# A two-layer pixelwise kernel: column stage in two 64x64 tiles, and regions of 13 row tiles for 15

## The chip, the cores and the metric

The kernel runs on one core of a Trainium2 chip. The metric is the device time of one execution in microseconds (us), lower is better. Engines are named as the profile names them: PE (TensorE matmuls), PEld (its weight loads), DVE (VectorE), ACT (ScalarE), POOL (GpSimd), SP (SyncE, which here only issues DMAs).

## What is computed

```
x: (1, 16, 1024, 1024)                      # 16 channels, rows t, columns s, float32
# first layer: a bias that depends on the distance t - s alone
rel  = tril(t - s)
nd   = log(|c * rel| + 1) / (log(|c * max(rel_max(t), threshold)| + 1) + 1e-6)
bias = relu(nd * W1 + b1) @ W2 + b2         # 32 hidden values to 16 channels
y    = x + bias
# second layer: channel mixing, part of it by row, part by column
A[t] = w + I + sum_i qw1[t,i] (x) qw2[t,i] + diag(qdd[t])     # 16 x 16 for each row t
B[s] =         sum_i kw1[s,i] (x) kw2[s,i] + diag(kdd[s])     # 16 x 16 for each column s
out[:, t, s] = A[t]^T y[:, t, s] + B[s]^T y[:, t, s]
```

## The kernel before

**Layout.** The 1024 columns are 8 blocks of W = 128. The 128 partitions are 8 blocks times 16 channels, in four groups of 32: two blocks' channels interleaved (GS = 2). A *row tile* is 8 rows by all columns, 128 x 1024 values; there are 128. Row tiles are taken in 9 *regions* of 8 and then 15 tiles (`REGION_TILES`). The buffer `homes` has three homes of 15 tiles: x of one region is loaded one tile behind the place where y is then written, and the mixed result of a region goes into another home.

**Work of a region k**, in steps:

- 16 *column tiles* (`b_columns`, L736): 8 columns each. For each column a 16x16 matrix acts on the 120 rows of the region. Two blocks' matrices stand as a 32x32 block-diagonal weight in `mats_b`, one matmul for each of the four groups, at the array's four diagonal 32x32 tiles: 32 matmuls of 32x32 weights and 120 columns to a column tile. Float32 makes each matmul two records in the profile, each with a weight load.
- then 15 *row tiles* (`a_rows`, L723), the same with the row's matrices from `mats_a`, 32 matmuls of 128 columns.
- in between, at the steps that `bias_step` gives (about every second), one *bias tile* (`bias_tile`, L747) of region k + 1: the hidden values of 8 rows, which GpSimd multiplies (L451) and ScalarE passes through Relu (L490), times W2, four matmuls of 512 columns with one hidden tile (first half of the rows) and eight records, so twice as many, with two.

Column sums are written out of the PSUM tile `main` by ScalarE on even steps (`take_b`, L517) and VectorE on odd ones (L629), row results are added by VectorE (`finish_tile`, L639), and VectorE adds the bias to x (`add_bias`, L657); in the first half of the rows ScalarE does half of the x partitions (L501). `main` has two halves, so TensorE can be at most two tiles ahead of those who empty it. Each engine runs its program strictly as written.

**The queues.** SP issues all loads of x, in pieces (`LOAD_PIECES`, 15 tiles as 1, 3, 3, 3, 4, 1, numbered from 0, each as 8 DMAs, one for each block), the row matrices (`load_mats_a`, four DMAs, which wait until GpSimd has spread an earlier set, L428), and half of the stores (`store_upper`, four DMAs of a piece of `STORE_PIECES`, behind the last row tile of the piece). ScalarE issues the other half of the stores. What stands in SP's program in the loop over k and T (L374 to L397): pieces 3 and 4 of region k + 1 first; then, by row tile T of region k, a_mats, piece 5 of region k + 1 at T = 6, the stores, and pieces 0, 1, 2 of region k + 2 at T = 7, 10, 13. An instruction that waits holds up all behind it.

**Start.** b's matrices are made by VectorE, transposed by TensorE, written out by SP and loaded back into `mats_b` (L336), which ScalarE fills with zeros before (L484).

Of the kernel before, what the change touches and what calls it, by code (L numbers as in the profile page):

```python
# [5 lines left out]
ACT = mybir.ActivationFunctionType  # L6

P = 128
H = 16
S = 1024  # L10
W = 128
BLOCKS = S // W
GS = 2
GROUPS = BLOCKS // GS
GP = H * GS
HID = 32
SLOTS = P // HID
ROWS = 8
COLS = ROWS * W
COL_TILES = W // ROWS  # L20
BANK = 512
REGION_TILES = (8,) + (15,) * 8
REGIONS = len(REGION_TILES)
FIRST_TILE = [sum(REGION_TILES[:k]) for k in range(REGIONS)]
ALL_TILES = S // ROWS
HALF_TILES = ALL_TILES // 2
HOME_TILES = max(REGION_TILES)
HOMES = 3
STORE_PIECES = {8: (2, 3, 3), 15: (2, 3, 3, 3, 4)}
LAST_STORES = (2, 3, 3, 3, 2, 1, 1)  # L30
LOAD_PIECES = {8: (1, 3, 4), 15: (1, 3, 3, 3, 4, 1)}
PORTIONS = (2, 2)
CHUNK = 32
CHUNK_TILES = CHUNK // ROWS
# [6 lines left out]
RING = 3  # L41
# [12 lines left out]
def build(nc, x, W1, b1, W2, b2, c, L_mult, init_L, qw1, qw2, kw1, kw2, qdd, kdd, w, out):  # L54
# [6 lines left out]
    with ExitStack() as ctx:  # L61
        def sb(name, shape):
            return ctx.enter_context(nc.sbuf_tensor(name, shape, F32))

        def sem(name):
            return ctx.enter_context(nc.semaphore(name))
# [2 lines left out]


        homes = sb("homes", [P, HOMES * HOME_TILES * COLS])
        mats_b = sb("mats_b", [P, GS * H * W])


        mats_in = sb("mats_in", [P, A_RING * H * CHUNK])
# [10 lines left out]
        zero_col = sb("zero_col", [P, 1])  # L86
# [53 lines left out]
        y_const_ready = sem("y_const_ready")  # L140
        main_ready = sem("main_ready")
        main_taken = [sem(f"main_taken{i}") for i in range(2)]
        out_done = [sem(f"out_done{i}") for i in range(len(LAST_STORES))]

        def tile_of(k, T):
            return FIRST_TILE[k] + T
# [1 line left out]
        def groups_of(u):  # L148
            return 1 if u < HALF_TILES else 2
# [70 lines left out]
        def load_pieces(k):  # L220
            return LOAD_PIECES[REGION_TILES[k]]

# [9 lines left out]
        def y_slot(k, T):  # L232
            return k % HOMES * HOME_TILES + T
# [24 lines left out]
        def of_block(tensor, pitch, b, offset, dims):  # L258
            start = (b // GS) * GP + b % GS
            return bass.AP(tensor, start * pitch + offset, [[GS * pitch, H]] + dims)  # L260
# [38 lines left out]
        def _(sp):  # L299
# [33 lines left out]

            def load_mats_b():
                for b in range(BLOCKS):
                    sp.dma_start(of_block(mats_b, GS * H * W, b, b % GS * W, [[GS * W, H], [1, W]]),  # L336
                                 b_mats[b]).then_inc(b_in, DMA)

            def save_mats(part):
# [18 lines left out]
            load_x(0, 2)  # L358
            save_mats("b")
            sp.wait_ge(mats_out["b"], 2 * DMA)  # L360
            sp.wait_ge(mats_zeroed, 1)
            load_mats_b()
            for i in range(3):
                load_x(1, i)
# [8 lines left out]
            loaded = [3, 5] + [0] * (REGIONS - 2)  # L373
            for k in range(REGIONS):  # L374

                while k + 1 < REGIONS and loaded[k + 1] < 5:
                    load_x(k + 1, loaded[k + 1])
                    loaded[k + 1] += 1
                if k == 2:
                    sp.wait_ge(scales_out, DMA)  # L380
                    sp.wait_ge(nd_ready, PART // 2 // ROWS)
                    sp.dma_start(row_scale[:, 0:PART // 2], late_scales[:, 0:PART // 2]).then_inc(scales_in, DMA)
                if k == 4:
                    sp.wait_ge(nd_ready, PART // ROWS)
                    sp.dma_start(row_scale[:, PART // 2:], late_scales[:, PART // 2:]).then_inc(scales_in, DMA)
                for T in range(REGION_TILES[k]):
                    v = chunk_behind(tile_of(k, T))
                    if v is not None:
                        load_mats_a(v)
                    if k + 1 < REGIONS and T == min(6, REGION_TILES[k] - 4):  # L390
                        load_x(k + 1, 5)
                    for i in range(len(store_pieces(k))):
                        if T == piece_start(store_pieces(k), i + 1) - 1 - (i == 4 and k < REGIONS - 1):
                            store_upper(k, i)
                    if k + 2 < REGIONS and T in (7, 10, 13):
                        load_x(k + 2, loaded[k + 2])
                        loaded[k + 2] += 1  # L397
            for i in range(len(out_done)):
# [3 lines left out]
        def _(pool):  # L402
# [30 lines left out]
            for u in range(ALL_TILES):  # L433
                t0 = u * ROWS
                if t0 == W:
                    pool.wait_ge(tables_made, 2)
                if t0 == PART:
                    pool.wait_ge(scales_in, DMA)
                if t0 == PART + PART // 2:
                    pool.wait_ge(scales_in, 2 * DMA)  # L440
                for g in range(groups_of(u)):
                    h = hidden_index(u, g)

                    while h >= RING and spread < UNITS and place_of_unit(spread) <= place_of_bias(tile_of_hidden[h - RING]):
                        spread_unit(spread)
                        spread += 1
                    if h >= RING:
                        pool.wait_ge(hidden_used, h - RING + 1)
                    logs = log_table[:, t0 - SLOTS * W * g:t0 - SLOTS * W * g + ROWS]
                    scales = row_scale[:, t0 % PART:t0 % PART + ROWS]  # L450
                    nc.gpsimd.tensor_tensor(  # L451
                        hidden_tile(u, g).rearrange("p (j s) -> p j s", j=ROWS),
                        bass.AP(logs.tensor, logs.offset, [list(logs.ap[0]), [1, ROWS], [1, W]]),
                        bass.AP(scales.tensor, scales.offset, [list(scales.ap[0]), [1, ROWS], [0, W]]),
                        ALU.mult).then_inc(nd_ready, 1)
# [5 lines left out]
        def _(act):  # L461
# [17 lines left out]
            for part in (row_scale[:, W:], scale_late):  # L479
# [1 line left out]
            act.wait_ge(w1_in, 2 * DMA)  # L481
            act.wait_ge(table_loaded, 1)
            nc.scalar.activation(relu_b1[:], b1_col[:], ACT.Relu).then_inc(relu_b1_made, 1)
            nc.scalar.activation(mats_b[:], zero_col[:].to_broadcast([P, GS * H * W]), ACT.Copy)\  # L484
                .then_inc(mats_zeroed, 1)

            def make_hidden(u):
# [193 lines left out]
        def _(pe):  # L681
# [19 lines left out]
            def of_group(g):  # L701
                return slice(GP * g, GP * (g + 1))

            def staggered(j, g):

                return (j + (ROWS // 2) * (g % 2)) % ROWS
# [2 lines left out]
                pitch = 2 * A_UNIT  # L709
                return bass.AP(mats_a, GP * g * pitch + w % 2 * A_UNIT + row, [[pitch, GP], [UNIT, GP]])  # L710

            def b_weights(g, col):
                return bass.AP(mats_b, GP * g * GP * W + col, [[GP * W, GP], [W, GP]])

            def y_row(k, T, g, j):
                at = y_slot(k, T) * COLS + j // 2 * 2 * W
                return homes[of_group(g), at:at + 2 * W].rearrange("p (s b) -> p s b", b=2)[:, :, j % 2]

            def y_column(k, g, col):
                rows = homes[of_group(g), y_slot(k, 0) * COLS:y_slot(k, REGION_TILES[k]) * COLS]  # L720
                return rows.rearrange("p (j s b) -> p j s b", s=W, b=2)[:, :, col, :]

            def a_rows(k, T):  # L723
# [12 lines left out]
            def b_columns(k, C):  # L736
                i = b_tile(k, C)
                taken, count = emptied(i - 2)
                pe.wait_ge(taken, count)
                for n in range(ROWS):  # L740
                    for g in range(GROUPS):
                        j = staggered(n, g)
                        mm = pe.matmul(main[of_group(g), i % 2, j * W:j * W + REGION_TILES[k] * ROWS],  # L743
                                       b_weights(g, C * ROWS + j), y_column(k, g, C * ROWS + j), start=True, stop=True)
                mm.then_inc(main_ready, 1)

            def bias_tile(u):  # L747
# [58 lines left out]
```

## Time and profile before

| | us |
|---|---|
| median of 3 runs | 911.75 |
| lowest and highest | 904.46, 914.53 |
| span of the profiled execution, first to last instruction | 930.2 |
| TensorE busy in it | 741.4 |
| GpSimd, VectorE, ScalarE busy | 432.9, 452.3, 387.6 |
| DMA traffic | 149.63 MB, 161 GB/s on average |

The profiled execution has no time of its own in the list beside its span. The span is 18.5 us over the median of the runs. Shares of the span are averages over stages with different limits. "issue" as the reason of an idle time means that the engine waited for nothing that the profile shows.

### The profile page before, as it was taken

How to read it: one execution, taken by the hardware profiler on the slowest of the kernel's cores; microseconds unless marked ns; L12 is line 12 of the kernel's file. 1: busy time of each engine (PE TensorE's matmuls, PEld its weight loads, DVE VectorE, ACT ScalarE, POOL GpSimd, SP SyncE). 2: the span in 40 equal slices, each digit the busy share in tenths (PEclk: the TensorE clock that was granted, in tenths of full speed). 3: DMA queues.
4: the chain of work that ended last, by engine and by line, in shares of the span. 5: the costliest groups of instructions: out<-in, count | busy, mean ns of one | idle time of the engine just before them, and what ended most of it. 6: DMA issues, size and time to landing. Idle time of an engine off the chain costs nothing. (4 is left out here: it accounts for less than half of the span.)

```text
span 930.2 us, 39085 instructions
## 1 busy us (share of the span) xinstructions
PE 741.4 (80%) x18210; PEld 547.7 (59%) x18210; DVE 452.3 (49%) x483; ACT 387.6 (42%) x412; POOL 432.9 (47%) x267
## 2 busy tenths in 40 slices
PE   0678864798678876898799978999689878897984
PEld 0255654576556655666557745677357645676974
DVE  7496522376345533564346524464336524464352
ACT  3958624553463435543433334344233342341200
POOL 3545421254233432365458745586358753581020
PEclk9888887999999999999999999999899988999997
DMA  6787687658975999587976898488875988589068
GB/s 132 183 172 140 147 180 167 145 100 190 194 180 125 183 184 201 124 183 161 223 156 129 174 181 192 94 172 172 182 162 110 199 178 151 106 176 227 5 155 200
DMA packets 301055, 149.63 MB, mean 161 GB/s; under 512 B 30045, under 2 KB 296669, under 8 KB 300893
## 3 DMA queue, kind: packets, MB, share of 16 engines
q1 hardware_dynamic: 231456, 113.56, 56.9%
q10 hardware_dynamic: 69436, 33.58, 17.0%
q8 instruction: 143, 2.34, 1.1%
q14 instruction: 20, 0.16, 0.1%
HBM read 77.61 MB, written 69.47 MB: 158 GB/s over the span
## 5 line engine op out<-in xcount | busy, mean ns | idle before, releaser
L451 POOL TENSOR_TENSOR hidden<-log_table,row_scale 128x1024 f32<-128x1024 f32 x192 | 365.4, 1917 | 367.4 <-PE bias L757 359.5
L743 PE MATMUL main<-homes,mats_b 32*32 32x120 f32 (+1 forms) x9216 | 286.5, 272 | 119.6 <-issue 83.3
L743 PEld LDWEIGHTS main<-homes,mats_b 32*32 32x32 f32 x9216 | 257.9, 133 | 187.5 <-issue 136.1
L490 ACT ACTIVATE hidden<-hidden,b_col 128x1024 f32<-128x1024 f32 x192 | 220.3, 1149 | 310.3 <-POOL hidden L451 205.1
L732 PEld LDWEIGHTS main<-homes,mats_a 32*32 32x32 f32 x8192 | 238.1, 129 | 78.6 <-issue 54.9
L732 PE MATMUL main<-homes,mats_a 32*32 32x128 f32 x8192 | 258.8, 275 | 23.7 <-issue 23.6
L657 DVE SCALAR_TENSOR_TENSOR homes<-bias,b_col,homes 64x512 f32<-64x512 f32 (+1 forms) x256 | 185.8, 747 | 174.9 <-DMA homes<-in_x 106.5
L757 PE MATMUL bias<-hidden,w_blocks 128*64 128x512 f32 x768 | 207.6, 648 | 17.7 <-DVE b_col L620 8.8
L639 DVE TENSOR_TENSOR homes<-main,homes 128x1024 f32<-128x1024 f32 x128 | 156.8, 1225 | 107.7 <-PE main L732 104.6
L629 DVE COPY homes<-main 128x960 f32<-128x960 f32 x64 | 74.1, 1157 | 179.7 <-PE main L743 179.5
L517 ACT ACTIVATE homes<-main 128x960 f32<-128x960 f32 (+1 forms) x80 | 71.1, 891 | 109.4 <-PE main L743 99.3
L428 POOL TENSOR_TENSOR mats_a<-mats_in,own_block 128x512 f32<-128x512 f32 x64 | 66.5, 1040 | 107.4 <-PE main L732 96.7
L501 ACT ACTIVATE homes<-homes,b_col 64x512 f32<-64x512 f32 x128 | 89.4, 749 | 64.5 <-DMA homes<-in_x 54.1
L757 PEld LDWEIGHTS bias<-hidden,w_blocks 128*64 128x64 f32 x768 | 46.4, 143 | 86.6 <-issue 74.6
L697 PE MATMUL bias<-relu_b,w_blocks 128*64 128x1 f32 x2 | 0.3, 241 | 15.1 <-DVE w_blocks L614 15.1
L290 DVE TENSOR_TENSOR homes<-homes 128x2048 f32<-128x2048 f32 x4 | 10.6, 2698 | 0.1
L697 PEld LDWEIGHTS bias<-relu_b,w_blocks 128*64 128x64 f32 x2 | 0.3, 204 | 15.1 <-issue 15.1
L691 PE MATMUL main<-homes 128*128 128x128 f32 x32 | 6.5, 389 | 3.0 <-DVE homes L594 3.0
L691 PEld LDWEIGHTS main<-homes 128*128 128x128 f32 x32 | 5.9, 206 | 4.8 <-DVE homes L594 3.2
L589 DVE TENSOR_TENSOR homes<-homes 128x2048 f32<-128x2048 f32 x2 | 6.2, 3110 | 0.1
L509 ACT ACTIVATE homes<-main 128x1024 f32<-128x1024 f32 x4 | 4.1, 1025 | 2.1 <-PE main L691 2.1
L473 ACT ACT_TABLE_LOAD x1 | 1.3, 1283 | 7.5 <-issue 7.5
(37 smaller groups left out, 32.2 us busy)
## 6 DMA issues: line engine op xcount, KB each, us to landing
homes<-in_x SPq DMA_DIRECT2D x200, 192.0 KB, 6.5
out_mixed<-homes ACTq DMA_DIRECT2D x104, 192.0 KB, 5.9
out_mixed<-homes SPq DMA_DIRECT2D x104, 192.0 KB, 5.6
homes<-in_x SPq DMA_DIRECT2D x72, 256.0 KB, 7.1
homes<-in_x SPq DMA_DIRECT2D x136, 64.0 KB
mats_in<-a_mats SPq DMA_DIRECT2D x128, 64.0 KB
out_mixed<-homes ACTq DMA_DIRECT2D x28, 256.0 KB, 8.0
out_mixed<-homes SPq DMA_DIRECT2D x28, 256.0 KB, 5.8
```

The source lines that it names most:

```text
L428: nc.gpsimd.tensor_tensor(mats_a[:, w % 2 * A_UNIT:(w % 2 + 1) * A_UNIT].rearrange("p (n b e) -> p n b e", n=H, b=GS), rows.unsqueeze(2).t ...
L451: nc.gpsimd.tensor_tensor(hidden_tile(u, g).rearrange("p (j s) -> p j s", j=ROWS), bass.AP(logs.tensor, logs.offset, [list(logs.ap[0]), [1 ...
L490: nc.scalar.activation(hidden_tile(u, g), hidden_tile(u, g), ACT.Relu, bias=b1_col[:, 0:1])\
L501: add = nc.scalar.activation(y_rows(high_half, k, T, b), x_rows(high_half, k, T, b), ACT.Identity, bias=b2_col[high_half, 1:2])
L517: nc.scalar.activation(mixed_columns(k, C), column_sums(k, C), ACT.Copy)\
L629: dve.tensor_copy(mixed_columns(k, C), column_sums(k, C)).then_inc(main_taken[b_tile(k, C) % 2], 1)
L639: dve.tensor_tensor(at, main[:, i % 2, :], at, ALU.add).then_inc(main_taken[i % 2], 1)
L657: add = dve.scalar_tensor_tensor(out=y_rows(rows, k, T, b), in0=falling(u, b, 0 if both else b * (P // 2), P if both else P // 2), scalar= ...
L691: mm = pe.transpose(main[:, i % 2, b * P:(b + 1) * P], comp[part][:, at:at + P], ident)
L732: mm = pe.matmul(main[of_group(g), i % 2, j * W:(j + 1) * W], a_weights(g, w, part * ROWS + j), y_row(k, T, g, j), start=True, stop=True)
L743: mm = pe.matmul(main[of_group(g), i % 2, j * W:j * W + REGION_TILES[k] * ROWS], b_weights(g, C * ROWS + j), y_column(k, g, C * ROWS + j), ...
L757: mm = pe.matmul(bias[into, u % 2, b * BANK:(b + 1) * BANK], w2_blocks[:, g, :], rows, start=True, stop=True)
```

## The change

The column stage works on four blocks at a time. `mats_b` holds 64x64 block-diagonal matrices (two groups' blocks, 4 x 16 channels), twice as large, and a column tile is 16 matmuls of 64x64 weights at the array's two diagonal 64x64 tiles. The row stage stays at 32x32. A home has 13 tiles: the regions are 6, nine times 13, and 5 tiles, eleven in all, with load and store pieces to match. ScalarE fills one half of `mats_b` with zeros as before, GpSimd the other half, ahead of its fourth hidden tile, and the load of the matrices waits for both. The second scale load stands at region 5 for 4.

```diff
+QS = 4
+QUADS = BLOCKS // QS
+QP = H * QS
-REGION_TILES = (8,) + (15,) * 8
+REGION_TILES = (6,) + (13,) * 9 + (5,)
-STORE_PIECES = {8: (2, 3, 3), 15: (2, 3, 3, 3, 4)}
-LAST_STORES = (2, 3, 3, 3, 2, 1, 1)
-LOAD_PIECES = {8: (1, 3, 4), 15: (1, 3, 3, 3, 4, 1)}
+STORE_PIECES = {6: (2, 2, 2), 13: (2, 3, 3, 3, 2)}
+LAST_STORES = (2, 1, 1, 1)
+LOAD_PIECES = {6: (1, 2, 3), 13: (1, 3, 3, 3, 2, 1), 5: (1, 2, 2)}
...
-        mats_b = sb("mats_b", [P, GS * H * W])
+        mats_b = sb("mats_b", [P, QP * W])
...
-                    sp.dma_start(of_block(mats_b, GS * H * W, b, b % GS * W, [[GS * W, H], [1, W]]),
+                    sp.dma_start(of_block(mats_b, QP * W, b, (b % QS // GS * GP + b % GS) * W, [[GS * W, H], [1, W]]),
...
-                while k + 1 < REGIONS and loaded[k + 1] < 5:
+                while k + 1 < REGIONS and loaded[k + 1] < min(5, len(load_pieces(k + 1))):
...
-                if k == 4:
+                if k == 5:
...
-                    if k + 1 < REGIONS and T == min(6, REGION_TILES[k] - 4):
+                    if k + 1 < REGIONS and len(load_pieces(k + 1)) > 5 and T == min(6, REGION_TILES[k] - 2):
...
-                    if k + 2 < REGIONS and T in (7, 10, 13):
+                    if k + 2 < REGIONS and T in (7, 10, 12):
...
+                if u == RING:
+                    nc.gpsimd.memset(mats_b[:, GP * W:], 0.0).then_inc(mats_zeroed, 1)
...
-            nc.scalar.activation(mats_b[:], zero_col[:].to_broadcast([P, GS * H * W]), ACT.Copy)\
+            nc.scalar.activation(mats_b[:, 0:GP * W], zero_col[:].to_broadcast([P, GP * W]), ACT.Copy)\
...
-            def b_weights(g, col):
-                return bass.AP(mats_b, GP * g * GP * W + col, [[GP * W, GP], [W, GP]])
+            def b_weights(q, col):
+                return bass.AP(mats_b, QP * q * QP * W + col, [[QP * W, QP], [W, QP]])
...
-                    for g in range(GROUPS):
-                        j = staggered(n, g)
-                        mm = pe.matmul(main[of_group(g), i % 2, j * W:j * W + REGION_TILES[k] * ROWS],
-                                       b_weights(g, C * ROWS + j), y_column(k, g, C * ROWS + j), start=True, stop=True)
+                    for q in range(QUADS):
+                        j = staggered(n, q)
+                        mm = pe.matmul(main[of_quad(q), i % 2, j * W:j * W + REGION_TILES[k] * ROWS],
+                                       b_weights(q, C * ROWS + j), y_column(k, q, C * ROWS + j), start=True, stop=True)
```

SP's program, before, from the a_mats load that stands ahead of piece 5 (`16x8x128 x8` is a piece of one tile) to pieces 2 and 3; row 65 is piece 1:

```order
59 L325 DMA mats_in<-a_mats 32x1x512 x4
60 L317 DMA homes<-in_x 16x8x128 x8
61 L268 DMA out_mixed<-homes 16x24x128 x4
62 L317 DMA homes<-in_x 16x8x128 x8
63 L325 DMA mats_in<-a_mats 32x1x512 x4
64 L268 DMA out_mixed<-homes 16x24x128 x4
65 L317 DMA homes<-in_x 16x24x128 x8
66 L325 DMA mats_in<-a_mats 32x1x512 x4
67 L268 DMA out_mixed<-homes 16x32x128 x4
68 L317 DMA homes<-in_x 16x24x128 x16
```

The same place in the changed program (line numbers are four higher); row 63 is piece 1:

```order
57 L272 DMA out_mixed<-homes 16x24x128 x4
58 L321 DMA homes<-in_x 16x8x128 x8
59 L329 DMA mats_in<-a_mats 32x1x512 x4
60 L272 DMA out_mixed<-homes 16x24x128 x4
61 L321 DMA homes<-in_x 16x8x128 x8
62 L272 DMA out_mixed<-homes 16x24x128 x4
63 L321 DMA homes<-in_x 16x24x128 x8
64 L329 DMA mats_in<-a_mats 32x1x512 x4
65 L272 DMA out_mixed<-homes 16x16x128 x4
66 L321 DMA homes<-in_x 16x24x128 x16
```

Between piece 5 and piece 1 the kinds and counts are the same; only the last store piece (row 67, now 65) is two tiles for four.

TensorE's program in a column stage, before (a row here is a matmul of the program, two records in the profile):

```order
70 L743 MATMUL main<-homes,mats_b 32x120 x64
71 L757 MATMUL bias<-hidden,w_blocks 64x512 x2
72 L743 MATMUL main<-homes,mats_b 32x120 x64
73 L757 MATMUL bias<-hidden,w_blocks 64x512 x2
74 L743 MATMUL main<-homes,mats_b 32x120 x64
```

and in the changed program, to the first row tile of the region:

```order
70 L752 MATMUL main<-homes,mats_b 64x104 x32
71 L766 MATMUL bias<-hidden,w_blocks 64x512 x2
72 L752 MATMUL main<-homes,mats_b 64x104 x32
73 L766 MATMUL bias<-hidden,w_blocks 64x512 x2
74 L752 MATMUL main<-homes,mats_b 64x104 x48
75 L766 MATMUL bias<-hidden,w_blocks 64x512 x2
76 L752 MATMUL main<-homes,mats_b 64x104 x16
77 L741 MATMUL main<-homes,mats_a 32x128 x32
```

Half as many matmuls stand between two bias tiles, and now and then three column tiles for two.

## Rows read from the trace of the kernel before

**Rows 1.** The page: engines, busy us; a DMA queue, packets, MB, share
```profile
PE 741.4 (80%) x18210; PEld 547.7 (59%) x18210; DVE 452.3 (49%) x483; ACT 387.6 (42%) x412; POOL 432.9 (47%) x267
...
q8 instruction: 143, 2.34, 1.1%
```

**Rows 2.** Windows: rows of region 5; columns of region 6; last rows
```profile
594.00:635.50 41.50, 41.50 (x1021) 30.51 (x1023) 28.43 (x30) 16.10 (x14) 35.40 (x22) 1.00 0.71 152
635.50:696.90 61.40, 49.12 (x1099) 32.65 (x1091) 20.17 (x23) 24.53 (x24) 28.42 (x16) 0.92 0.80 171
882.00:920.60 38.60, 30.95 (x961) 29.29 (x960) 18.31 (x15) 0.00 (x0) 6.24 (x6) 0.96 0.77 170
```

**Rows 3.** Timeline of TensorE in the last row stage
```profile
894.95 3.94 PE L732 MATMUL main<-homes,mats_a 32*32 32x128 f32 x127 [1.40 <-issue]
```

**Rows 4.** Waits: who for whom, us in total, times, longest
```profile
PE main L743 <- issue: 83.3, 45, 4.7
DVE homes L657 <- DMA homes<-in_x: 106.5, 13, 14.8
```

**Rows 5.** Timeline of VectorE: its second bias tile in four regions
```profile
155.39 1.51 DVE L657 SCALAR_TENSOR_TENSOR homes<-bias,b_col,homes 64x512 f32<-64x512 f32 x2 [7.20 <-DMA homes<-in_x]
...
453.06 1.41 DVE L657 SCALAR_TENSOR_TENSOR homes<-bias,b_col,homes 128x512 f32<-128x512 f32 x2 [10.30 <-DMA homes<-in_x]
...
660.69 1.41 DVE L657 SCALAR_TENSOR_TENSOR homes<-bias,b_col,homes 128x512 f32<-128x512 f32 x2 [14.80 <-DMA homes<-in_x]
...
765.83 1.41 DVE L657 SCALAR_TENSOR_TENSOR homes<-bias,b_col,homes 128x512 f32<-128x512 f32 x2 [13.85 <-DMA homes<-in_x]
```

**Rows 6.** Timeline of the SP queue: start, us, line, transfer, count
```profile
408.56 6.61 SPq L317 DMA_DIRECT2D homes<-in_x  x8
...
431.49 13.58 SPq L317 DMA_DIRECT2D homes<-in_x  x8
...
452.58 25.39 SPq L317 DMA_DIRECT2D homes<-in_x  x24
...
613.62 6.92 SPq L317 DMA_DIRECT2D homes<-in_x  x8
```

**Rows 7.** DMA of the stretch 431 to 478 us
```profile
DMA packets 17987, 9.17 MB, mean 195 GB/s; under 512 B 714, under 2 KB 17842, under 8 KB 17980
```

**Rows 8.** Timeline of TensorE in the column stage of region 4
```profile
431.07 3.64 PE L743 MATMUL main<-homes,mats_b 32*32 32x120 f32 x128
...
444.65 3.29 PE L743 MATMUL main<-homes,mats_b 32*32 32x120 f32 x116 [0.66 <-issue]
...
452.51 1.86 PE L743 MATMUL main<-homes,mats_b 32*32 32x120 f32 x60 [2.35 <-issue]
...
457.44 1.94 PE L757 MATMUL bias<-hidden,w_blocks 128*64 128x512 f32 x8
...
465.00 3.44 PE L757 MATMUL bias<-hidden,w_blocks 128*64 128x512 f32 x8
...
487.57 3.86 PE L732 MATMUL main<-homes,mats_a 32*32 32x128 f32 x128
```

**Rows 9.** Windows, TensorE: us, busy (records), clock, DMA share, GB/s
```profile
433.00:441.00 8.00, 6.85 (x190) 1.00 0.55 70
859.00:863.00 4.00, 3.83 (x80) 0.50 0.07 19
870.40:880.40 10.00, 10.00 (x397) 1.00 0.02 5
```

**Rows 10.** Timeline of TensorE: a column tile of 64 columns
```profile
57.66 1.12 PE L743 MATMUL main<-homes,mats_b 32*32 32x64 f32 x64
```

**Rows 11.** Timeline of the start: fill of mats_b, hidden tiles
```profile
11.55 3.60 ACT L484 ACTIVATE mats_b<-zero_col 128x4096 f32<-128x4096 f32 x1
...
26.30 1.90 POOL L451 TENSOR_TENSOR hidden<-log_table,row_scale 128x1024 f32<-128x1024 f32 x1 [9.45 <-PE bias L757]
...
28.89 1.90 POOL L451 TENSOR_TENSOR hidden<-log_table,row_scale 128x1024 f32<-128x1024 f32 x1 [0.69 <-PE bias L757]
```

More of the change, by code:

```diff
@@ L28 @@
 HOMES = 3
-STORE_PIECES = {8: (2, 3, 3), 15: (2, 3, 3, 3, 4)}
-LAST_STORES = (2, 3, 3, 3, 2, 1, 1)
-LOAD_PIECES = {8: (1, 3, 4), 15: (1, 3, 3, 3, 4, 1)}
+STORE_PIECES = {6: (2, 2, 2), 13: (2, 3, 3, 3, 2)}
+LAST_STORES = (2, 1, 1, 1)
+LOAD_PIECES = {6: (1, 2, 3), 13: (1, 3, 3, 3, 2, 1), 5: (1, 2, 2)}
+MOST_STORES = max(len(LAST_STORES), max(len(v) for v in STORE_PIECES.values()))
 PORTIONS = (2, 2)
@@ L142, in build @@
         main_taken = [sem(f"main_taken{i}") for i in range(2)]
-        out_done = [sem(f"out_done{i}") for i in range(len(LAST_STORES))]
+        out_done = [sem(f"out_done{i}") for i in range(MOST_STORES)]
         def tile_of(k, T):
@@ L360, in _ @@
             sp.wait_ge(mats_out["b"], 2 * DMA)
-            sp.wait_ge(mats_zeroed, 1)
+            sp.wait_ge(mats_zeroed, 2)
             load_mats_b()
@@ L710, in a_weights, with of_quad @@
                 return bass.AP(mats_a, GP * g * pitch + w % 2 * A_UNIT + row, [[pitch, GP], [UNIT, GP]])
-            def b_weights(g, col):
-                return bass.AP(mats_b, GP * g * GP * W + col, [[GP * W, GP], [W, GP]])
+            def of_quad(q):
+                return slice(QP * q, QP * (q + 1))
+            def b_weights(q, col):
+                return bass.AP(mats_b, QP * q * QP * W + col, [[QP * W, QP], [W, QP]])
             def y_row(k, T, g, j):
@@ L717, in y_row, with y_column @@
                 return homes[of_group(g), at:at + 2 * W].rearrange("p (s b) -> p s b", b=2)[:, :, j % 2]
-            def y_column(k, g, col):
-                rows = homes[of_group(g), y_slot(k, 0) * COLS:y_slot(k, REGION_TILES[k]) * COLS]
+            def y_column(k, q, col):
+                rows = homes[of_quad(q), y_slot(k, 0) * COLS:y_slot(k, REGION_TILES[k]) * COLS]
                 return rows.rearrange("p (j s b) -> p j s b", s=W, b=2)[:, :, col, :]
```

## The prediction

> **What bounds the kernel now.** I read the page first, then the windows by stage, the waits, and last the queues. TensorE is busy 80% [rows 1], so it looks like the bound. The windows correct that: a row stage takes 41.5 us for 15 tiles with TensorE busy throughout, but a column stage 61.4 us with TensorE busy 49.1 [rows 2]. The time to be had lies in the column stages, and two things take it.
>
> The first is instruction supply. "issue" gaps come 127 or 128 matmul records apart (894.95 is the first of five in a row), and a record has its weight load beside it: 256 instructions. Queue 8 moved 143 packets with 2.34 MB, 16 KB each [rows 1, 3]. So TensorE's program arrives in pieces of 256 instructions, and in heavy traffic a piece comes late. The waits put 83.3 us on that at L743 [rows 4]. The Trainium skill ("Runtime: NRT & Kernel Launch", Instruction fetch mechanics) describes the 16 KB refills and calls a crossing mostly hidden; the size agrees with this trace, the hiding does not.
>
> The second is x. VectorE waits 106.5 us for it [rows 4]. In every column stage from region 1 on it stands 7 to 15 us at its second bias tile [rows 5], and the column sums that it should empty stand behind that. What it wants there is load piece 1 (tiles 1 to 3) of the next region. The SP queue shows why it is late: piece 5 goes out at 408.56, then without a hole a store, piece 0, a_mats, a store, and at 431.49 piece 1, whose eight DMAs take 13.58 us to issue; it is used at 453.06 [rows 5, 6], and the DMA moves 195 GB/s meanwhile [rows 7]. From piece 5 to use this is 44.5 us; two regions on, 613.62 to 660.69, 47.1.
>
> So a region is a loop, and I count it from one use of piece 1 to the next. From 155.39 to 765.83 there are six, 101.7 us each; the first three, mostly with one hidden tile for each bias tile, 99.2, the last three, with two, 104.3 [rows 5]. Three parts follow one another. Part **a**, use of piece 1 to the first row tile: 34.5 us (453.06 to 487.57), and 36.2 (660.69 to 696.9) [rows 2, 5, 8]. Part **b**, first row tile to the issue of piece 5, which SP reaches only behind stores and a_mats loads that wait for row tiles 1 to 6: 613.62 - 594 = 19.6 us [rows 2, 6], and 24.0 as what is left of the mean loop; 22.7 taken. Part **c**, 45. Together 103 to 104. A check: the second hidden tile costs TensorE about half of 1.94 us at each of 15 bias tiles [rows 8], 14 us a loop, and the loop grew by 5. Work of TensorE counts in part a alone.
>
> **The change, part by part.**
> *Column tile.* 16 matmuls of 64x64 with 104 columns stand for 32 of 32x32 with 120 (32 records for 64). Four 32-wide blocks work side by side before, two 64-wide ones after, so each block does 16 records a tile either way and the time goes by columns. 64 columns: 1.0 us a tile (1.12 with the last one's end) [rows 10]. 120: 397 records in 10.0 us, 1.61 a tile [rows 9]; in the bias pattern 3.64 for two, with ends and switches 1.75 [rows 8]. On the line between 1.0 and 1.75, 104 columns make 1.53; in proportion to the free stream 1.40. I take 1.48, a saving of 0.27. The 64-wide weight load I take as hidden, as bias matmuls with weights of that width run eight in 1.94 us [rows 8].
> The Trainium skill ("TensorE: Matmul & The Clock Gate", LDWEIGHTS) gives a load's columns over 1.2 GHz, by which 32 columns are 27 ns and 64 are 53. Were loads in series by that rule, a tile would be 1.71 us before and after. Records with 32-wide weights start under 18 ns apart here [rows 10], so this trace doesn't bear it out.
> *Instruction supply.* Two column tiles and a bias tile are 272 instructions in 5.5 us before, 144 in 5.0 after: a piece of 256 lasts 5.2 us now and 8.9 then. Late pieces come up to 7.9 us after one another (444.65, 452.51) [rows 8], so nearly all stalls of the column stages go. But those ahead of piece 1 hide a wait that is there anyway. Behind it, part a is 34.5 us, and without stalls would be 2.5 (until VectorE has caught up) + 9 column tiles x 1.75 + 5 bias tiles x 2.0 = 28.3: 6 us a loop to be had (one bias tile of 3.44 for 1.94 is in it [rows 8]), not the 10 that 83.3 us over nine regions suggest.
> *Regions.* 13 tiles for 15, so the loops run from region 2 to region 10: eight, not six.
> Part a: nine column tiles at 1.48, 13.3; bias tiles T=3 to 6, 8.0; catching up 2.5: 24. Piece 2 is issued some 8.5 us behind piece 1 and its store (25.39 for three pieces [rows 6]), lands about 14 after it, and TensorE now wants it after 11: +1. TensorE also stands some 18 us for piece 1 now instead of a few, and after such a stand the granted clock is 0.50 for a while (859 to 863) [rows 9]: +1.5. So a = 26.5, or 25 with one hidden tile. Bounds: 22, all hidden, and 31, as before less two bias tiles.
> Part b: the same gates at the same row rate, 22.7 and 21.5.
> Part c: the same 36 DMAs in the same order (SP's rows in the section on the change); ScalarE's stores beside them shrink by 2 tiles in 4 blocks, 0.52 MB, 2.6 us at 195 GB/s: 42.5. Bounds: 38, if the slow stretch at 433 to 441, 70 GB/s [rows 9], is passed over, and 45.
> Loop: 91.7, with one hidden tile 89. That is 7.0 us per row tile; 104.3/15 is 6.95. The loop shrinks by 12%, the region by 13%.
> *Start.* Region 0 has 6 tiles for 8, and bias tiles there come 2.6 us apart [rows 11]: 5 us sooner, so the first use (155.4) comes at 150.5. GpSimd's fill of the new half of mats_b stands before its fourth hidden tile, which waits 9.45 us for TensorE; ScalarE's fill of that size took 3.60, and at GpSimd's 1.9 us for 1024 elements it would be 7.6 [rows 11]: covered. Without the cover it costs those 3.6 to 7.6 once.
> *End.* Region 10's piece 1 has 2 tiles, 2 us less. Behind its use, 5 column tiles, a bias tile and the catching up, 12; 13 row tiles at 1.82 (half of 3.64, the row pair 3.86 with its end) and two bias tiles, 28. Region 10: 16 column tiles of 40 columns at 0.6 to 1.0, 13; 5 row tiles, 9; late instructions, 3. Stores behind the last row tile, 930.2 - 920.6 = 9.6 [rows 2].
> The two scale loads move by a region and nobody waits for them; switches from 64-wide to 32-wide blocks lie in the 1.48.
>
> **Sum.** 150.5 + (3 x 89 + 90.5 + 4 x 91.7) - 2 + 40 + 25 + 9.6 = 947 us against the span of 930.2: +17. The median of the runs, 911.75, lies 18 us under that span; I carry the difference over: 911.75 + 17 = 929 us. A measurement of this kernel can't tell 1% from no change.
>
> **Rivals.** (1) *The loop goes by bytes, not by order.* 13 tiles of x and output and 3.25 sets of a_mats are 14.5 MB; at 195 GB/s 74 us [rows 7], and 5 to the first gate make 80: 11 less than mine, eight times, span 860, time 842. For it: the DMA is at its limit in the burst. Against: between bursts SP stood and waited for row tiles, as it still must. Chance 0.28, from 825 to 900.
> (2) *They balance.* With c at 40, loops are some 2.4 us shorter: span 928, time 910. Chance 0.20.
> (3) *Slower still: the 64-wide load shows.* If part of the 25 ns between 32-wide records is the load, a 64-wide record takes up to 54 ns and a tile stays 1.75: 2.4 us a loop, 19 in all, and the short tiles of regions 0 and 10 take 1.7 for 0.8, 29 more: time 977. It decides once a load is over 45 ns. Against it: under 18 ns at 64 columns. Chance 0.05.
> My forecast, 921 to 955, has 0.47.
>
> **How the numbers follow.** Slower by over 1%: 0.47 + 0.05 = 0.52. Within 1%: 0.20. Faster: 0.28. The range leaves out rival 3 and the lower half of rival 1: 862 to 958. The likeliest case's own is 921 to 955; a, b and c all at their bounds (22, 19.6, 38 and 31, 24.0, 45) would make the loop 80 or 100 us.
>
> **What would show it.** Right: L743's issue waits fall from 83 us to under 25; VectorE's wait for x grows from 106.5 to 150 or more; the eight uses of piece 1 stand some 91 us apart; unhindered 64x64 tiles take 1.40 to 1.55 us. Wrong: uses 80 us apart mean that the queue's order wasn't the bound; waits for piece 1 under 10 us mean that part c has shrunk; records of 64x64 over 50 ns apart mean that the load shows.

## The result, and the profile after

| | before | changed |
|---|---|---|
| median of 4 timed runs, us | 908.69 (904.46 to 914.53) | 961.61 (959.36 to 964.23) |
| profiled execution: own time, span, us | own time not known, span 930.2 | 964.23, span 962.4 |

The ratio is 1.059 (95% interval 1.052 to 1.067): the change costs 53 us where 17 were forecast, and 961.6 lies just above the range's end of 958. On another chip the changed kernel took 962.47, the kernel before 923.36, and the ratio was 1.042 (1.036 to 1.048).

The page of the changed kernel answers to [rows 1]: first the engines, then queue 8. TensorE has 3584 matmul records fewer and is busy longer, its weight loads too. Queue 8 moved 115 packets for 143.

```profile
PE 795.6 (83%) x14626; PEld 620.4 (64%) x14626; DVE 454.4 (47%) x499; ACT 390.9 (41%) x428; POOL 437.3 (45%) x268
...
q8 instruction: 115, 1.88, 0.9%
```

The waits (who for whom, us in total, times, longest) answer to [rows 4]. The column line is L752 now, and instruction supply is no longer listed among its waits: those 83.3 us are gone. At the row line L741 supply still costs 15.4 us. What TensorE waits for is ScalarE and VectorE, which empty column sums, and VectorE stands 170.9 us for x, up from 106.5.

```profile
PE main L752 <- ACT homes L523: 48.3, 14, 12.0
PE main L752 <- DVE homes L635: 39.7, 5, 11.1
PE main L741 <- issue: 15.4, 14, 2.5
...
DVE homes L663 <- DMA homes<-in_x: 170.9, 26, 15.2
```

VectorE's timeline at the first use of piece 1 in regions 2, 6, 7 and 10 answers to [rows 5]. From 143.67 to 859.90 there are eight loops of 89.5 us. The stand in the brackets is 12 to 15 us in all nine uses but the first and the last. The nine add up to 103 us of the 170.9. Before, the seven uses were 77 of 106.5, so more than half of what was added is for other pieces, often for piece 0, on which VectorE stands some 5 us at its first bias tile of a column stage.

```profile
143.67 1.51 DVE L663 SCALAR_TENSOR_TENSOR homes<-bias,b_col,homes 64x512 f32<-64x512 f32 x2 [5.59 <-DMA homes<-in_x]
...
491.85 1.41 DVE L663 SCALAR_TENSOR_TENSOR homes<-bias,b_col,homes 128x512 f32<-128x512 f32 x2 [13.85 <-DMA homes<-in_x]
...
585.90 1.41 DVE L663 SCALAR_TENSOR_TENSOR homes<-bias,b_col,homes 128x512 f32<-128x512 f32 x2 [15.15 <-DMA homes<-in_x]
...
859.90 1.41 DVE L663 SCALAR_TENSOR_TENSOR homes<-bias,b_col,homes 128x512 f32<-128x512 f32 x2 [2.24 <-DMA homes<-in_x]
```

The SP queue (start, us, line, transfer, count) answers to [rows 6]: piece 5 at 453.13, a store, piece 0, a_mats, a store, and at 477.40 piece 1, whose use is the row at 491.85 above. From piece 5 to use this is 38.7 us; it was 44.5.

```profile
453.13 6.21 SPq L321 DMA_DIRECT2D homes<-in_x  x8
459.38 4.46 SPq L272 DMA_DIRECT2D out_mixed<-homes  x4
463.88 7.42 SPq L321 DMA_DIRECT2D homes<-in_x  x8
471.35 3.31 SPq L329 DMA_DIRECT2D mats_in<-a_mats  x4
474.70 2.65 SPq L272 DMA_DIRECT2D out_mixed<-homes  x4
477.40 9.45 SPq L321 DMA_DIRECT2D homes<-in_x  x8
```

TensorE's timeline answers to [rows 8]. A pair of column tiles, 64 records, takes 3.77 us beside other work, against 3.64 for 128 records before. The gap of 9.77 us is the wait for piece 1, handed on by VectorE's evictions. The last row is region 10: 16 column tiles of 40 columns in 28.60 us, 1.78 each.

```profile
471.33 3.77 PE L752 MATMUL main<-homes,mats_b 64*64 64x104 f32 x64
482.46 2.01 PE L752 MATMUL main<-homes,mats_b 64*64 64x104 f32 x32
494.24 3.04 PE L752 MATMUL main<-homes,mats_b 64*64 64x104 f32 x32 [9.77 <-DVE homes L635]
505.12 3.77 PE L752 MATMUL main<-homes,mats_b 64*64 64x104 f32 x64
...
520.57 2.04 PE L741 MATMUL main<-homes,mats_a 32*32 32x128 f32 x64
...
911.41 28.60 PE L752 MATMUL main<-homes,mats_b 64*64 64x40 f32 x512
```

The windows (us, then busy us and instructions of PE, PEld, DVE, ACT and POOL, granted clock, DMA share, GB/s) answer to [rows 2, 9]: columns of region 5, rows of region 5, the end of region 9's columns, and region 10's columns. The last two rows have 104 columns at a granted clock of 1.00 and 40 columns at 0.55, mostly the lower of its two levels. The first has 160 records in 8.90 us, 56 ns each; the second 512 in 28.5, 56 ns again. Neither the clock nor the number of columns shows. The weight load beside the matmul is busy throughout, 8.83 of 8.90 and 28.45 of 28.50, but that alone proves nothing: it was so before as well, at 120 columns and 25 ns a record (the last row below, from the kernel before). That 104 and 40 columns cost the same is the sign of the load.

```profile
465.60:520.60 55.00, 44.96 (x576) 33.70 (x572) 18.00 (x22) 22.98 (x23) 27.58 (x17) 0.91 0.76 171
520.60:558.40 37.80, 36.37 (x884) 26.49 (x882) 24.25 (x26) 13.88 (x13) 28.92 (x19) 1.00 0.61 148
...
862.50:871.40 8.90, 8.90 (x160) 8.83 (x160) 2.93 (x3) 1.73 (x2) 0.00 (x0) 1.00 0.43 106
...
911.40:939.90 28.50, 28.50 (x516) 28.45 (x512) 4.67 (x8) 3.50 (x8) 0.00 (x0) 0.55 0.19 43
```

```profile
870.40:880.40 10.00, 10.00 (x397) 9.96 (x392) 3.47 (x3) 2.95 (x4) 0.00 (x0) 1.00 0.02 5
```

### The profile page after: what moved, and what is told of

The parts are those of the page before. It is cut to its first block and busy times, and to the rows that moved or that the text cites. A ratio compares the mean times of both kernels' runs of the same rounds, so it can differ in the third digit from the quotient of the medians.

```text
span 962.4 us, 32082 instructions
## 1 busy us (share of the span) xinstructions
PE 795.6 (83%) x14626; PEld 620.4 (64%) x14626; DVE 454.4 (47%) x499; ACT 390.9 (41%) x428; POOL 437.3 (45%) x268
## 5 line engine op out<-in xcount | busy, mean ns | idle before, releaser
L752 PEld LDWEIGHTS main<-homes,mats_b 64*64 64x64 f32 x5632 | 335.2, 203 | 168.4 <-ACT homes L523 58.0
L752 PE MATMUL main<-homes,mats_b 64*64 64x104 f32 (+2 forms) x5632 | 351.0, 284 | 105.0 <-ACT homes L523 48.3
L663 DVE SCALAR_TENSOR_TENSOR homes<-bias,b_col,homes 64x512 f32<-64x512 f32 (+1 forms) x256 | 185.9, 747 | 256.0 <-DMA homes<-in_x 170.9
L741 PEld LDWEIGHTS main<-homes,mats_a 32*32 32x32 f32 x8192 | 235.0, 128 | 64.9 <-issue 42.3
L741 PE MATMUL main<-homes,mats_a 32*32 32x128 f32 x8192 | 255.9, 273 | 15.5 <-issue 15.4
L766 PE MATMUL bias<-hidden,w_blocks 128*64 128x512 f32 x768 | 200.3, 629 | 13.7 <-DVE b_col L626 8.8
L635 DVE COPY homes<-main 128x832 f32<-128x832 f32 (+1 forms) x80 | 77.7, 971 | 140.7 <-PE main L752 140.5
L523 ACT ACTIVATE homes<-main 128x832 f32<-128x832 f32 (+2 forms) x96 | 73.0, 761 | 123.3 <-PE main L752 116.9
L432 POOL TENSOR_TENSOR mats_a<-mats_in,own_block 128x512 f32<-128x512 f32 x64 | 66.6, 1041 | 89.5 <-PE main L741 87.5
L766 PEld LDWEIGHTS bias<-hidden,w_blocks 128*64 128x64 f32 x768 | 45.0, 139 | 73.9 <-issue 56.5
```

The lines of the kernel that those rows point to most:

```text
L432: nc.gpsimd.tensor_tensor(mats_a[:, w % 2 * A_UNIT:(w % 2 + 1) * A_UNIT].rearrange("p (n b e) -> p n b e", n=H, b=GS), rows.unsqueeze(2).t ...
L523: nc.scalar.activation(mixed_columns(k, C), column_sums(k, C), ACT.Copy)\
L635: dve.tensor_copy(mixed_columns(k, C), column_sums(k, C)).then_inc(main_taken[b_tile(k, C) % 2], 1)
L663: add = dve.scalar_tensor_tensor(out=y_rows(rows, k, T, b), in0=falling(u, b, 0 if both else b * (P // 2), P if both else P // 2), scalar= ...
L741: mm = pe.matmul(main[of_group(g), i % 2, j * W:(j + 1) * W], a_weights(g, w, part * ROWS + j), y_row(k, T, g, j), start=True, stop=True)
L752: mm = pe.matmul(main[of_quad(q), i % 2, j * W:j * W + REGION_TILES[k] * ROWS], b_weights(q, C * ROWS + j), y_column(k, q, C * ROWS + j), ...
```

## The experiments

Kernels that ran together have the same time of the kernel before beside them: it was 909.11 us for e0 to e3, 931.08 for e4 to e7, and 923.36 for e8 to e10. So between these groups ratios are compared, not times.

**e0: the kernel before once more, for its trace.** No edit.

> The kernel before, unchanged, for a second profile. Theory A (the first profiled execution was about 20 us longer than the executions that were timed, and the 18 us carried over in the prediction were an accident of that one execution): the span comes out at 902 to 913 us, some 2 us under the execution's own time, and the loops from one use of piece 1 to the next average 98 to 99 us, not 101.7. Rival: profiling lengthens this kernel in every execution: span near 930.

It took 912.93 us, span 911.1. Against the execution that the prediction was made on, the waits at the column line are 65.4 us for 83.3. The seven uses of piece 1 stand 100.05 us apart, from 153.87 to 754.19, for 101.7; 98 to 99 was expected. The 930.2 us were one long execution: of its 19 us more, 10 lie in the six loops and 8 behind the last of them.

```profile
DVE homes L657 <- DMA homes<-in_x: 115.7, 13, 14.9
...
PE main L743 <- issue: 65.4, 41, 4.8
```

**e1: the regions alone.** The changed kernel, with column sums in four 32x32 tiles again:

```diff
-                    for q in range(QUADS):
-                        j = staggered(n, q)
+                    for g in range(GROUPS):
+                        j = staggered(n, g)
...
-                return bass.AP(mats_b, QP * q * QP * W + col, [[QP * W, QP], [W, QP]])
+                return bass.AP(mats_b, GP * g * QP * W + g % 2 * GP * W + col, [[GP * W, GP], [W, GP]])
```

> The changed kernel with its column tiles taken back to 32 matmuls of 32x32 (regions of 13 tiles, pieces, mats_b and its fills as changed). Theory A (regions cost through the fixed part of each loop, and the 64-wide tiles cost on top as their weight load shows): 930 to 948 us, the last region's 16 column tiles in 12 to 15 us for 28.5, issue waits at the column line back at 50 us or more. Rival B (the regions are the whole loss, the tiles are neutral): 955 to 965 us. Rival C (the tiles are the whole loss): 905 to 918 us.

991.38 us, ratio 1.090 (1.080 to 1.100). No theory had this: short regions alone cost 82 us, more than the whole change. Its TensorE waits show that instruction supply costs at least what it did before (85.9 us, for 65.4 in e0 and 83.3 in the first trace), and its waits for x have grown as in the changed kernel.

```profile
DVE homes L663 <- DMA homes<-in_x: 157.4, 25, 17.3
...
PE main L752 <- issue: 85.9, 51, 5.1
```

Its timeline of TensorE in region 10 shows supply by itself. 128 records, two column tiles, take 2.36 us, 18 ns each, and then the next piece is missing, every 3.47 us, at 5 GB/s of DMA traffic. Here even an undisturbed fetch is slower than TensorE. The 16 column tiles of region 10 take 30.7 us in this way, more than the 28.5 of the changed kernel.

```profile
951.27 2.36 PE L752 MATMUL main<-homes,mats_b 32*32 32x40 f32 x128 [1.12 <-issue]
954.74 2.36 PE L752 MATMUL main<-homes,mats_b 32*32 32x40 f32 x128 [1.11 <-issue]
```

The window over these column tiles (columns as above):

```profile
938.00:968.70 30.70, 18.64 (x1029) 17.35 (x1020) 4.67 (x8) 3.50 (x8) 0.00 (x0) 0.59 0.25 60
```

**e2: the tiles alone.** The kernel before, with column sums in two 64x64 tiles. The wide matrices don't fit beside homes of 15 tiles, so weights are read at half the step from the small ones, and the column sums are of other weights:

```diff
-            def b_weights(g, col):
-                return bass.AP(mats_b, GP * g * GP * W + col, [[GP * W, GP], [W, GP]])
+            def b_weights(q, col):
+                return bass.AP(mats_b, 2 * GP * q * GP * W + col // 2, [[GP * W, 2 * GP], [W // 2, 2 * GP]])
```

> The kernel before with column tiles of 16 matmuls of 64x64, and everything else as before (regions of 15). There is no room for the 64x64 matrices there, so the weights are read with half the step out of the small mats_b: the sums of the column stage are not the reference's, the instructions, sizes and places are. Theory A (a 64-wide record takes 55 to 58 ns for its weights, a tile 1.85 us, at 120 columns as at 104; the instruction stalls go, the wait for piece 1 takes their place): 905 to 925 us, column records 55 to 58 ns apart, no issue waits over 15 us at the column line, the last region's column tiles in 28 to 30 us for 26. Rival B (tiles neutral in themselves, instruction supply was worth something): 880 to 900 us. Rival C (tiles are the whole loss of 53 us): 950 or more.

867.37 us, ratio 0.954 (0.945 to 0.962): better than any theory had it, and with a column tile that is no faster. Its waits at the column line are 26.5 and 23.0 us for evictions, with supply gone from it; VectorE's wait for x is about as before.

```profile
DVE homes L657 <- DMA homes<-in_x: 104.7, 14, 15.6
...
PE main L746 <- ACT homes L517: 26.5, 6, 9.7
PE main L735 <- issue: 24.5, 19, 3.4
PE main L746 <- DVE homes L629: 23.0, 5, 9.8
```

Its timeline of TensorE in the last region: 448 records with 120 columns in 25.30 us, 56.5 ns each, 1.81 us a tile, where [rows 9] has 397 narrow records in 10.0 us, 25 ns each and 1.61 a tile.

```profile
797.66 25.30 PE L746 MATMUL main<-homes,mats_b 64*64 64x120 f32 x448 [0.28 <-ACT homes L517]
```

The two halves and the whole, each by one profiled execution, in us. "Start" is the first use of piece 1; a is from a use to the first row tile; b + c from there to the next use; "end" is what follows the last use that is counted (region 8's for regions of 15 tiles, region 9's for 13):

| | start | loops | a | b + c | end | span |
|---|---|---|---|---|---|---|
| 32x32, regions of 15 (e0) | 153.9 | 6 x 100.1 | 34.8 | 65.3 | 156.9 | 911.1 |
| 64x64, regions of 15 (e2) | 148.2 | 6 x 93.6 | 29.1 | 64.5 | 161.5 | 871.0 |
| 32x32, regions of 13 (e1) | 151.3 | 7 x 91.6 | 29.5 | 62.1 | 201.0 | 993.2 |
| 64x64, regions of 13 (changed) | 143.7 | 7 x 89.7 | 27.7 | 62.0 | 191.1 | 962.4 |

Read down the columns. The tiles act on part a, 5.7 us a loop with 15 tiles and 1.8 with 13. Parts b and c hardly move: 65.3, 64.5, 62.1, 62.0. A region two tiles shorter is worth 3 us there, and there are two regions more. With narrow tiles the loop is 8.5% shorter (100.1 to 91.6) for 13% fewer row tiles.

**e3: what a 64-wide tile costs.** The changed kernel; in the last region alone, each quarter of the column stage has another form, from 64 rows by 64 weight columns through 32 by 32, 64 by 32 and 32 by 64. That region's sums are of other blocks in three of them:

```diff
+                form = C // 4 if k == REGIONS - 1 else 0
...
+                        if form == 0:
+                            into, of, wide, first = of_quad(r), of_quad(r), QP, QP * r
+                        elif form == 1:
+                            into, of, wide, first = of_group(r), of_group(r), GP, GP * r
+                        elif form == 2:
+                            into, of, wide, first = of_group(r), of_quad(r // 2), GP, QP * (r // 2)
+                        else:
+                            into, of, wide, first = of_quad(r), of_group(2 * r), QP, QP * r
```

> The changed kernel with four forms of the column matmul in its last region, four column tiles each, 40 columns, where nothing else runs beside TensorE: 64 rows deep and 64 wide in two tiles of the array, 32x32 in four, 64 deep and 32 wide in four, 32 deep and 64 wide in two. The last region's sums are not the reference's in three of the four forms. Theory A1 (a load costs by its width, one at a time, whatever tile it goes to): 55, 27, 27 and 55 ns a record. A2 (a load costs by its width and loads into different 32-row strips go side by side): 55, 15 or less, 27, and 55 halved. A3 (the stream of 40 columns or the issue is the bound): all under 20 ns, which the 55 ns of the first form already speaks against.

It took 955.99 us in the one run. The timeline of TensorE has the forms one after another, 40 columns each. At 64 rows by 32 columns, 128 records take the same 2.36 us as at 32 by 32.

```profile
912.80 2.36 PE L765 MATMUL main<-homes,mats_b 32*32 32x40 f32 x128 [0.91 <-issue]
916.54 2.57 PE L765 MATMUL main<-homes,mats_b 32*32 32x40 f32 x128 [1.39 <-issue]
920.29 2.36 PE L765 MATMUL main<-homes,mats_b 64*32 64x40 f32 x128 [1.17 <-issue]
```

The weight loads grouped by form in 902 to 932 us (behind the names the weights' rows*columns, then count, busy us, mean ns) sort them. 7.2 us for 128 or 126 loads of 64 columns are 56 to 57 ns each, whether the weights have 32 rows or 64; 4.6 us for 256 loads of 32 columns are 18 ns, again with 32 rows or 64.

```profile
L765 PEld LDWEIGHTS main<-homes,mats_b 32*64 32x64 f32 x128 | 7.2, 198 | 0.1
L765 PEld LDWEIGHTS main<-homes,mats_b 64*64 64x64 f32 x126 | 7.2, 200 | 0.5 <-ACT homes L523 0.5
L765 PEld LDWEIGHTS main<-homes,mats_b 64*32 64x32 f32 x256 | 4.6, 163 | 2.9 <-issue 2.8
L765 PEld LDWEIGHTS main<-homes,mats_b 32*32 32x32 f32 x256 | 4.6, 163 | 2.6 <-issue 2.5
```

So the rows of the weights don't matter, and the 64-wide forms cost three times as much a record as the 32-wide. Two things change together between them, the width and the number of array tiles that the records take in turn: two of 64, four of 32. No run separates these, so that a single load costs by its width alone is not shown; for this change they come together in any case. A column tile has 32 records in the wide form, 32 x 57 = 1.82 us, at 40, 104 and 120 columns alike. Both theories had parts of this and neither both numbers.

**e4 and e5: piece 1 earlier in the SP queue,** two row tiles sooner, in the kernel before and in the changed one:

```diff
-                    if k + 2 < REGIONS and T in (7, 10, 12):
+                    if k + 2 < REGIONS and T in (7, 8, 12):
```

> The kernel before, with the x pieces of region k + 2 issued at T = 7, 8, 13 for 7, 10, 13: piece 1 goes out right behind piece 0, ahead of a_mats and of the fourth store. Theory A (the place of piece 1 in SP's queue sets the loop; part c is 44 us of 100): c shrinks by the 8 DMAs that no longer stand before it, 6 to 7 us, in six loops: 868 to 880 us for 909. Rival B (part c is bytes, the order matters not): 900 to 915 us, piece 1 landing where it landed.

> The changed kernel with the same edit, T = 7, 8, 12 for 7, 10, 12. Theory A: eight loops, 5 to 7 us each: 905 to 922 us for 961. Rival B: 955 to 965 us.

e4: 915.54 us, ratio 0.983 (0.975 to 0.991), between theory A's 3 to 4.5% and the rival's nothing. Its trace, of its longest execution (922.48), has 88.1 us of waits for x, for 115.7 in e0, and 74.9 us of instruction supply at the column line, between e0's 65.4 and the 83.3 of the first trace. e5: 925.17 us, ratio 0.996 (0.989 to 1.002), where the changed kernel without it stands at 1.042 to 1.059. The loops are 83.2 us for 89.7 (145.98 to 728.31, seven), and c is 33.3 for 39.9. The same edit gives the changed kernel 4.5 to 6%, as theory A had it (4 to 6% of 961), and the kernel before 1.7%. VectorE's rows in one column stage of e5 show what is late next: piece 1 is 5.37 us late for 13.85, and then piece 2 is 5.12 late.

```profile
472.85 1.41 DVE L663 SCALAR_TENSOR_TENSOR homes<-bias,b_col,homes 128x512 f32<-128x512 f32 x2 [5.37 <-DMA homes<-in_x]
...
490.80 1.42 DVE L663 SCALAR_TENSOR_TENSOR homes<-bias,b_col,homes 128x512 f32<-128x512 f32 x2 [5.12 <-DMA homes<-in_x]
```

**e6: short regions, homes of 15.** The kernel before with the changed list of regions and its pieces, everything else (small matrices, addresses, 32x32 tiles) as before:

```diff
-REGION_TILES = (8,) + (15,) * 8
+REGION_TILES = (6,) + (13,) * 9 + (5,)
-HOME_TILES = max(REGION_TILES)
+HOME_TILES = 15
```

> The kernel before with regions of 6, nine times 13, and 5 tiles and their pieces, but homes of 15 tiles and the small mats_b: the regions change, the memory of a home does not, and nothing of the mats_b part. Theory A (every region costs a loop of which two thirds do not depend on its tiles): as with the regions alone, 980 to 1000 us. Rival B (the loss of that kernel came from shorter homes, so less room for x, or from the larger mats_b and its fills): 905 to 950 us.

997.55 us, ratio 1.074 (1.066 to 1.081). So most of the loss comes with the list of regions and its pieces, not with the size of the homes, nor with the wide matrices and their fill. The number of regions and the shorter pieces were not varied one without the other.

**e7, e8 and e9: the rest of the pieces earlier too.** e7 is the kernel before and e8 the changed one, with T in (7, 8, 10); e9 is e8 with two tiles in piece 0 and two in piece 1, for one and three:

```diff
-LOAD_PIECES = {6: (1, 2, 3), 13: (1, 3, 3, 3, 2, 1), 5: (1, 2, 2)}
+LOAD_PIECES = {6: (1, 2, 3), 13: (2, 2, 3, 3, 2, 1), 5: (1, 2, 2)}
```

> The kernel before with T = 7, 8, 10: piece 1 as in the run with 7, 8, 13, and piece 2 early as well, ahead of the fifth store. Theory A: once piece 1 comes early, piece 2 is what VectorE waits for next, so this gains some 2 us a loop over it: 855 to 875 us. Rival: piece 2 goes ahead of stores that free the homes, and nothing more is gained: the same as with 7, 8, 13 within 8 us.

> The changed kernel with T = 7, 8, 10 for 7, 10, 12: pieces 1 and 2 early. With T = 7, 8, 12 VectorE stood some 5 us for piece 1 and again 4 to 6 us for piece 2 in each region. Theory A (queue order sets the loop, instruction supply no longer does with 64x64 tiles): VectorE's wait for x falls from 139 us to under 100, the ratio to the kernel before to 0.96 to 0.985. Rival (the DMA is full there by now, order gains nothing more): 0.99 to 1.00, as with 7, 8, 12.

> As the run with T = 7, 8, 10 on the changed kernel, and the load pieces 2, 2, 3, 3, 2, 1 for 1, 3, 3, 3, 2, 1, so that tile 1 comes with piece 0. Theory A: the second bias tile no longer waits for piece 1, another 1 to 3 us a loop: ratio to the kernel before 0.94 to 0.975. Rival (the bytes up to tile 3 are the same, and so is the wait for them, one tile later): within 1% of the run with 7, 8, 10.

e7: 920.02 us, ratio 0.991 (0.983 to 0.999), no better than e4. VectorE's wait for x is 50.8 us, half of before, and the time hasn't followed: supply stands at 76.0 us at the column line. The likely reading is that in that kernel one of the two takes the other's place. It isn't shown, as the kernel before was not traced on this chip. e8: 913.65 us, 0.989 (0.982 to 0.995); e9: 908.82 us, 0.986 (0.980 to 0.992), no different from it, as its rival had it. e8 fell between its theory (0.96 to 0.985, waits under 100 us) and its rival. Both beat the two kernels given; e4, the smallest edit, is as good as they are. The waits of e8 and of e9 for x, against 148.3 in e10 on the same chip and 170.9 at first:

```profile
DVE homes L663 <- DMA homes<-in_x: 119.4, 26, 11.7
```

```profile
DVE homes L663 <- DMA homes<-in_x: 93.6, 19, 11.6
```

**e10: the changed kernel again,** beside e8 and e9. No edit.

> The changed kernel as it is, on the chip of the two runs beside it, whose ratios need it as a measure. Ratio to the kernel before 1.05 to 1.07, as at first; VectorE's wait for x 160 us or more.

962.47 us, ratio 1.042 (1.036 to 1.048), beside 961.61 on the first chip. The kernel before moved 1.6% between the two, the changed one 0.1%. Both expectations of this run failed: 1.05 to 1.07, and a wait for x of 160 us or more. The size of the effect is thus +39 or +53 us; its sign is the same.

```profile
DVE homes L663 <- DMA homes<-in_x: 148.3, 22, 13.5
```

## Why the forecast had the sign and not the size

*The loop: right in kind, its length partly by luck.* A region is a round between SP's queue and the row tiles, of which most doesn't shrink with the tiles. Forecast were eight loops of 90.5 us, measured are 89.5; a 27.8 for 25 to 26.5, b 21.8 for 22.7 and 21.5, c 39.9 for 42.5. The errors of a and c cancel in part. Piece 5 to piece 1 goes out in the order that was given, and the four rows of the table in the experiments show b + c at 62 to 65 us under all four combinations. The experiments that move piece 1 forward (e4, e5) show that the order of the queue is a cause of it. Rival 1, a loop that goes by bytes, would have put the uses 80 us apart and is out. Rival 2's premise, c at 40, came true; its time of 910 us didn't, since part a and all that stands outside the loops took longer.

*Instruction supply in the column stage: right.* The forecast "under 25 us" for the column line's waits came out at next to nothing. e2 shows the price of it without the regions: 42 us (909.11 to 867.37), with a column tile that costs 1.81 us for 1.61. By the spans 39 of 40 us lie in the six loops, 6.5 each; the prediction gave supply 6 us a loop, and part a fell by 5.7 in e2 though its column tiles had become slower.

*The column tile: this step failed.* "The 64-wide weight load I take as hidden, as bias matmuls with weights of that width run eight in 1.94 us" [rows 8]. Those matmuls stream 512 columns and take 243 ns each, so a load of 57 ns doesn't show in them; records of 104 columns are 56 ns apart, and there it does. The tile takes 1.82 us alone and 1.85 in pairs, not 1.48, at 40 columns 1.78, not 0.6 to 1.0. The mechanism was rival 3's, with a chance of 0.05; the prediction's own sign for it, records of 64x64 over 50 ns apart, is what came. It was turned down because records with 32-wide weights start 18 ns apart, and e3 shows that this says nothing on 64: the cost is not in proportion. The Trainium skill ("TensorE: Matmul & The Clock Gate", LDWEIGHTS) gives a load's columns over 1.2 GHz and says that rows don't matter. As an estimate by it, 64 columns are 53 ns; e3 has 56 to 57 at 64 and at 32 rows (clock 0.50), the changed kernel 56 at a clock of 1.00, which agrees within 6%. By it 32 columns are an estimated 27 ns; e3 has 18 a record, over four array tiles in turn, which doesn't agree.

In terms of the sum, for the profiled execution's 962.4 against the 947 forecast:

| term | forecast | measured | difference |
|---|---|---|---|
| first use of piece 1 | 150.5 | 143.7 | -6.8 |
| eight loops (2 us off for region 10's short piece) | 722 | 716.2 | -6 |
| from the last use to region 10 | 40 | 51.5 | +11.5 |
| region 10 | 25 | 38.6 | +13.6 |
| last row tile to the end | 9.6 | 12.4 | +2.8 |

The two large terms lie where no wait for x hides TensorE. Region 10's columns take 28.5 us for 13: this is the 64-wide load. Narrow tiles would not have helped there, as e1 has 30.7 us for want of instructions. From the last use to the row tiles it is 15.4 us for 12, with column tiles that cost 1.85. The 13 row tiles of region 9 take 36.1 us for 28, and 5.8 of that are three gaps of instruction supply. The sum had nothing for them there; its 3 us for late instructions stood at region 10, where none came:

```profile
891.55 3.88 PE L741 MATMUL main<-homes,mats_a 32*32 32x128 f32 x127 [1.04 <-issue]
897.98 3.85 PE L741 MATMUL main<-homes,mats_a 32*32 32x128 f32 x127 [2.55 <-issue]
904.02 3.62 PE L741 MATMUL main<-homes,mats_a 32*32 32x128 f32 x61 [2.19 <-issue]
```

Within the loops the slow tile is mostly covered, since TensorE stands 10 us for piece 1 in any case: part a came out 1.3 to 2.8 us above its forecast.

*The carried difference: this step failed as well, and it is slightly the larger part of the miss.* Of the 33 us between 929 and 961.6, 15 lie in the span; the rest is "I carry the difference over". The 18 us between the profiled span and the median belonged to one long execution of the kernel before. The sum was taken against it, and then the changed kernel was given the same 18 us as a correction. e0's own time, 912.93, is within 4 us of the median, and the changed kernel's profiled execution within 3 us of its own. Taken against e0's span of 911.1, the forecast of 947 would have been +36.

*What the change is worth by halves.* From 909.11: tiles alone -42, regions alone +82, together +52 (961.61). So beside regions of 13 the tiles give 30 us (e1's 991.38 to 961.61), not 42. The table of spans has where: the start gives 8, seven loops 13, the end 10. In the loops most of the gain is lost: with 13 tiles one gains 1.9 us from the tiles, not 6.5. What the tiles save ahead of the use of piece 1 goes into the wait for it, the 9.77 us in TensorE's timeline above. That is argued from the trace; e5 bears it out, where an earlier piece 1 gives the changed kernel about three times what it gives the kernel before.

What stays open: why b + c is shorter by only 3 us with two row tiles fewer. Part b is 21.7 us in e0 and 21.8 in the changed kernel, part c 43.6 and 39.9. Part b ends at a gate that hangs on tiles 1 to 6 in both kernels, and part c goes by transfers, which fits; which transfers of c could still be shortened, no run here tells apart. Also open is why a record with 32-wide weights costs less than a third of one with 64-wide: it can be the load itself, or that loads for four array tiles overlap more than loads for two. Narrow weights taken in turn by two array tiles would tell.

## What to carry to other kernels

Before you make an outer step smaller, measure what each pass costs whatever its size. Here 62 of 90 us shrank by only 3 with the region, and two more regions, with shorter pieces, cost 82 us, where half the instructions of the column stage gave 42. That a load is hidden in one row says nothing of a shorter row: compare it with the shortest matmul that will stand over it, not with any matmul whose weights are as wide. And compare a profiled execution with the median of its kernel before a sum is made on it; where they differ by more than the effect, a second profile is worth more than a correction.

## What the runs showed that was not expected

- Records with 64-wide weights, in two array tiles, cost 56 to 58 ns, with 40, 104 or 120 columns streamed, at a granted clock of 0.50 as at 1.00. With 32-wide weights, in four, they cost 18 ns at 40 columns and 25 at 120. With 40 columns in e3, 32 or 64 rows of weights made no difference. A tile of the array comes round every 2 x 57 = 114 ns with wide weights, and every 4 x 18 = 72 ns (40 columns) or 4 x 25 = 100 ns (120 columns) with narrow ones. So the wide form halves the instructions and makes the matmuls themselves slower.
- Instruction supply binds even at 5 GB/s of DMA traffic: 256 instructions take 3.47 us in region 10 of e1, of which TensorE needs 2.36.
- Half the instructions in one stage gave 4.6% of the time (e2), with the stage's matmuls slower.
- The kernel before took 909 us on one chip, 923 and 931 on two others; the changed one 961.6 and 962.5.
